# Two graph blocks on one core: the left sums, the normalisation and three orders in the front

## What is computed

```
h = max(layernorm(x), 0)
type_sum_a = adj @ h ; type_sum_b = adj @ h
attn_a = sigmoid(concat(type_sum_a, h) @ Wa.T + ba)      # attn_b the same with Wb, bb
H = h @ W_sa
s_left, s_right = H @ a_sa[0, :256], H @ a_sa[0, 256:]
e = where(adj != 0, exp(-leaky_relu(s_left[:, None] + s_right[None, :], 0.01)), 0)
x_a = (e / (sum(e, 1) + 1e-5)) @ H
x_b = adj @ (h @ W_gcnb) + b_gcnb
x = x + sigmoid(attn_a * x_a + attn_b * x_b)
```

## Time and profile before

| | |
|---|---|
| median of 3 runs | 1577.26 us |
| the profiled execution, its own time | 1576.58 us |
| its span, first to last instruction | 1574.8 us |
| PE busy | 1542.0 us, 98% |
| DVE / ACT / POOL busy | 72% / 68% / 62% |
| granted TensorE clock, mean | 1.000 |

### The profile page before, as it was taken

The page is one execution under the profiler, slowest core; times in us unless marked ns, Lnnn a source line. Parts: engine busy times, 40 slices in busy tenths (PEclk is TensorE's granted clock), DMA queues, the critical chain, the costliest instruction groups (busy, mean ns, idle before and its releaser), DMA issues.

```text
span 1574.8 us, 34791 instructions
## 1 busy us (share of the span) xinstructions
PE 1542.0 (98%) x12902; PEld 1532.8 (97%) x12902; DVE 1138.9 (72%) x2145; ACT 1067.3 (68%) x2085; POOL 969.6 (62%) x864
## 2 busy tenths in 40 slices
PE   6999999999999999999999999999999999999998
PEld 5999999999999999999999999999999999999997
DVE  7766666666666577778777778766777777777774
ACT  4579889988985566666666666645666666666666
POOL 2112222222220288888888888846888888888885
PEclk9999999999999999999999999999999999999999
DMA  4124444454441034344444435522343344434343
GB/s 151 48 61 118 125 115 119 119 147 120 115 115 35 24 95 105 105 105 106 107 108 105 105 105 161 204 68 75 105 105 105 105 105 105 105 105 105 105 107 106
DMA packets 95034, 166.27 MB, mean 106 GB/s; under 512 B 12816, under 2 KB 25743, under 8 KB 94607
## 3 DMA queue, kind: packets, MB, share of 16 engines
q1 hardware_dynamic: 66816, 116.17, 27.2%
q0 software_dynamic: 24336, 44.31, 11.5%
q10 hardware_dynamic: 3710, 3.56, 0.7%
HBM read 150.87 MB, written 13.13 MB: 104 GB/s over the span
## 4 chain that ended last, share of the span: by engine, by line
PE 89%; issue 3%; DVE 3%; POOL 2%; ACT 1%; DMA 1%; SPq 0%; POOLq 0%; DVEq 0%; ACTq 0%
PE PS L1295 33%; PE PS L1507 9%; PE PS L1510 9%; PE PS L1509 9%; PE PS L1370 5%; PE PS L1367 5%; PE PS L1369 5%; PE PS L1368 5%; PE PS L1366 5%; POOL FR L508 1%; POOL X L501 1%; DVE ROW L837 0%; DVE AF L1104 0%; DMA X<-xt 0%; PE PS L1538 0%
## 5 line engine op out<-in xcount | busy, mean ns | idle before, releaser
L508 POOL TENSOR_TENSOR FR<-AF,FR 128x512 fp32r<-128x512 f32 x338 | 451.1, 1335 | 122.3 <-ACT FR L703 114.6
L1295 PE MATMUL PS<-FR,RB 128*128 128x256 f32 x3900 | 514.0, 281 | 1.8 <-ACT X L657 1.7
L1295 PEld LDWEIGHTS PS<-FR,RB 128*128 128x128 f32 x3900 | 481.9, 188 | 3.0 <-ACT X L657 3.0
L501 POOL TENSOR_TENSOR X<-X,ROW 128x512 f32<-128x512 f32 x283 | 370.7, 1310 | 82.0 <-ACT ROW L713 82.0
L1507 PE MATMUL PS<-FR,RA 128*128 128x256 f32 x1300 | 370.6, 285 | 2.5 <-POOL FR L508 2.3
L1510 PE MATMUL PS<-FR,RA 128*128 128x256 f32 x1300 | 365.0, 281 | 0.0
L1509 PE MATMUL PS<-FR,RA 128*128 128x256 f32 x1300 | 364.4, 280 | 0.0
L1104 DVE TENSOR_TENSOR AF<-PS,AJ 128x512 f32<-128x512 f32 x338 | 231.0, 683 | 56.3 <-ACT PS L669 46.2
L466 POOL DMA_DIRECT2D STGT<-adjt x169 | 90.1, 533 | 293.0 <-PE PS L1370 293.0
L1036 DVE TENSOR_TENSOR AF<-PS,AF 128x512 f32<-128x512 f32 x286 | 196.4, 687 | 100.7 <-PE PS L1295 98.4
L657 ACT ACTIVATE X<-PS 128x512 f32<-128x512 f32 x272 | 162.3, 597 | 156.4 <-DVE AF L1036 149.5
(11 more groups left out here) (174 smaller groups left out, 2424.1 us busy)
## 6 DMA issues: line engine op xcount, KB each, us to landing
AJ<-adjt SPq DMA_DIRECT2D x338, 256.0 KB, 2.7
STGT<-adjt POOLq DMA_DIRECT2D x169, 256.0 KB, 3.0
xt_scratch<-ROW SPq DMA_DIRECT2D x12, 512.0 KB, 2.6
RB<-xt_scratch SPq DMA_DIRECT2D x12, 512.0 KB, 6.2
x_scratch<-X ACTq DMA_DIRECT2D x13, 256.0 KB, 2.1
ROW<-x_scratch SPq DMA_DIRECT2D x13, 256.0 KB, 3.3
out<-ROW SPq DMA_DIRECT2D x12, 256.0 KB, 3.5
ROW<-rec_scratch SPq DMA_DIRECT2D x22, 128.0 KB, 3.7
```

The source lines that it names most:

```text
L501: nc.gpsimd.tensor_tensor(slot, slot, MB.unsqueeze(1).broadcast_to([P, 2, 256]), ALU.subtract)\
L508: nc.gpsimd.tensor_tensor(LO[g % 2], WA[g % 2], HI[g % 3].bitcast(F32), ALU.subtract)\
L1295: last = nc.tensor.matmul(out, stationary(a, k), moving(b, k), start=(k == 0 and i == 0), stop=(k == K - 1 and i == 2))
```

## The change

- **Left sums.** `products_l` goes, and WSL with it. The vector W_sa @ a_left becomes a fourth extra column of H's weights (HX was 260 already), so s_left comes out as a column of H's product, and `h2_low` copies four columns to XS instead of three. s_left then stands down the partitions and has to be laid along the free axis. For pair 0 that is done by ACT (`spread_left`), two transposes on PE (`turn_left`, bank 1) and a copy on ACT. For pairs 1 to 6 and 7 to 12 it is done by two stores of SL to DRAM and two loads back with the partitions broadcast, on SP's queue (`SL_PARTS`).
- **Banks.** `turn` hands out five turns a pair; transposes of pair 1 use bank 0.
- **Weight vectors.** The two sums go from DVE (reduce_sum) to ACT (four copies with an accumulated output, written into the weights).
- **Normalisation** of pairs 2 to 12 goes from DVE to POOL, between the powers and the loads of adjacency units. Pairs 0 and 1 stay on DVE.
- **x's second part** goes ahead of a_sa's rows on SP's queue; its statistics are taken in two parts. In the passes, statistics move ahead of `h2_low`.
- **Leaky steps.** In pass 1 `leaky0(0)` and `exp0(0)` come after G's high parts. After the loop, `leaky0(13)` is no longer issued right there; for units 11 to 13 the order is leaky n + 2, high n + 1, exp n + 2, then back to the old one. In pass 12 both copies of XS come before the low parts.

```diff
+SL_PARTS = [(1, 7), (7, PAIRS)]
+N_LATE = UNITS + 1
...
         def turn(pr, i):
-            return 6 * pr + i + 1 if i else max(6 * pr - 5, 0)
+            return 5 * pr + i + 1 if i else max(5 * pr - 4, 0)
...
             sp.dma_start(WRAW0[:, :, 0:GX + D + 2], wx).then_inc(w_in, 16)
+            sp.dma_start(X[:, X_PARTS[1][0]:X_PARTS[1][1], :], xt[:, X_PARTS[1][0]:X_PARTS[1][1], :])\
+              .then_inc(x_in[1], 16)
             sp.dma_start(AROW, rows[:, 0:2 * D]).then_inc(row_in, 16)
...
+            for i, (p0, p1) in enumerate(SL_PARTS):
+                sp.wait_ge(sr_done, 2 * p1)
+                sp.dma_start(sl_dram[2 * P * p0:2 * P * p1].rearrange("(t p o) -> p t o", p=P, o=1),
+                             SL[:, 2 * p0:2 * p1, :], allow_slow_non_contiguous=True).then_inc(sl_st, 16)
+                sp.wait_ge(sl_st, 16 * (i + 1))
+                sp.dma_start(SLB[:, 2 * P * p0:2 * P * p1],
+                             sl_dram[2 * P * p0:2 * P * p1].partition_broadcast(P)).then_inc(sl_in[i], 16)
...
             for n in range(NSTG):
                 load_unit(n)
-            for n in range(2, len(LN_PARTS)):
-                inverse_root(n, *LN_PARTS[n])
-            for n in range(UN - NSTG):
+            normalise(2)
+            for p in range(1, PAIRS - 2):
+                if p - 1 in LN_CHAIN:
+                    i = LN_CHAIN[p - 1]
+                    inverse_root(i, *LN_PARTS[i])
+                normalise(p + 2)
+                if p >= 2:
+                    load_unit(p - 2 + NSTG)
+            for n in range(PAIRS - 4, UN - NSTG):
...
+            def spread_left():
+                act.wait_ge(sr_done, 2)
+                nc.scalar.activation(PEB[:, :, 0:P], SL[:, 0:2, :].broadcast_to([P, 2, P]), ACT.Copy).then_inc(sl_spread, 1)
...
+                for k in range(K):
+                    wa = (PEB, PAB)[side][:, k, 0:D]
+                    last = nc.scalar.activation(wa, wa, ACT.Copy, accum_out=WRAW0[:, k, c:c + 1])
...
+                ahead = pr == PAIRS - 1
+                if not (ahead and h):
+                    dve.wait_ge(h2hi_done, t + 1 + ahead)
+                    for i in range(1 + ahead):
+                        nc.vector.tensor_copy(XS[:, t + i, :], PS[:, bank_of(pr, 3 + h + i), D:D + 4])\
+                          .then_inc(sr_done, 1)
...
-            def products_l(pr):
...
+            def turn_left():
+                pe.wait_ge(sl_spread, 1)
+                for h in range(2):
+                    last = nc.tensor.transpose(PS[:, 1, h * P:(h + 1) * P], PEB[:, h, 0:P], IDN[:, :])
+                last.then_inc(sl_mm, 1)
```

More of the change, by code:

```diff
@@ L212, in two_graph_blocks @@
         wv_zero = sem("wv_zero")
-        wv_step = sem("wv_step")
-        wsl_hi = sem("wsl_hi")
+        wv_done = sem("wv_done")
+        sl_spread = sem("sl_spread")
+        sl_mm = sem("sl_mm")
+        sl_first = sem("sl_first")
+        sl_st = sem("sl_st")
+        sl_in = [sem(f"sl_in{i}") for i in range(len(SL_PARTS))]
         wh_cast = sem("wh_cast")
@@ L471, in inverse_root, with normalise @@
                 nc.gpsimd.tensor_tensor(LNT[:, 1, t0:t1], LNT[:, 0, t0:t1], NHALF[:, 0:t1 - t0], ALU.pow)                  .then_inc(ln_pow, 1)
+            def normalise(pr):
+                pool.wait_ge(ln_done, next(i for i, (t0, t1) in enumerate(LN_PARTS) if 2 * pr + 1 < t1) + 1)
+                if pr:
+                    pool.wait_ge(tp_done, pr)
+                for h in range(2):
+                    t = 2 * pr + h
+                    last = nc.gpsimd.tensor_scalar(HN[:, h, :], X[:, t, :], RSTD[:, t:t + 1], NMR[:, t:t + 1],
+                                                   ALU.mult, ALU.add)
+                last.then_inc(hn_done, 1)
             pool.wait_ge(half_set, 1)
@@ L544, in leaky0 @@
                 pr, u = n // UNITS, n % UNITS
-                act.wait_ge(slb_done, pr + 1)
+                if pr == 0:
+                    act.wait_ge(sl_first, 1)
+                else:
+                    act.wait_ge(sl_in[next(i for i, (p0, p1) in enumerate(SL_PARTS) if pr < p1)], 16)
                 act.wait_ge(sr_done, 2 * u + 2)
@@ L601, in _ @@
             transposed_high(0)
-            act.wait_ge(wv_step, 1)
-            nc.scalar.activation(WSL[:, 0, :, :], WV[:, 0, :].unsqueeze(2).broadcast_to([P, K, P]), ACT.Copy)\
-              .then_inc(wsl_hi, 1)
-            act.wait_ge(wv_step, 3)
+            for side in range(2):
+                act.wait_ge(wv_pool, side + 1)
+                c = GX + D + 3 - side
+                for k in range(K):
+                    wa = (PEB, PAB)[side][:, k, 0:D]
+                    last = nc.scalar.activation(wa, wa, ACT.Copy, accum_out=WRAW0[:, k, c:c + 1])
+            last.then_inc(wv_done, 1)
+            act.wait_ge(wv_done, 1)
             act.wait_ge(wv_zero, 1)
@@ L956, in _ @@
             normalise(0)
+            dve.wait_ge(x_in[1], 16)
+            statistics(2, 4)
             dve.wait_ge(wg_hi, 1)
@@ L1002, in _ @@
                     statistics(t0, t1)
+                if p == 1:
+                    mask0(0)
+                h2_low(p, 0)
+                if p >= 1:
+                    low0(p - 1)
+                h2_low(p, 1)
                 if p in LN_CHAIN:
                     i = LN_CHAIN[p]
-                    variances(i, *LN_PARTS[i], 2 + sum(b <= LN_PARTS[i][1] for a, b in LN_STATS.values()))
+                    variances(i, *LN_PARTS[i], 3 + sum(b <= LN_PARTS[i][1] for a, b in LN_STATS.values()))
             mask0(UNITS - 1)
```

124 lines of the change are left out of this document (56 added, 68 removed).

## The result

| | before | after |
|---|---|---|
| median (4 runs each, same chip) | 1577.45 us (1576.45 to 1577.85) | 1568.12 us (1567.39 to 1568.53) |
| ratio, 95% interval | | 0.9943 (0.9927 to 0.9959) |
| profiled execution, its span | 1576.58, 1574.8 us | 1568.53, 1566.7 us |

The change is faster by 9.3 us (0.6%). The forecast was 15.65 us faster, and the time lies 1.1 us above the range. The profiled execution stands 0.4 us above the median. The mean granted TensorE clock was 1.00 in both profiles.

A forecast was written before the change was run, and what follows sets the result against it. TensorE, busy 98% of the span, was taken to bound the kernel. Savings of 8.1 (first passes), 5.6 (full passes) and 1.95 (end of the front), together 15.65, took 1577.26 to 1561.6 us; range 1558.5 to 1567.0.

The forecast's parts named there:

- unknown cost: Price of one 128x256 tensor_scalar on POOL, shown by no row: taken as 0.7 us, between 0.33 and 1.46.
- Term 3, the end of the front: PE's idle before unit 12, at 104.54 us, would vanish: -1.95 us.
- high to 3.7, low to 4.4: Times after the last H product for unit 12's high and low parts, under the 4.8 us PE has in units 10 and 11.
- now both copies come right behind the high parts: In pass 12, both XS copies would be done 0.8 us after the last H product.
- the rival on the store: Slow word stores of s_left make leaky 13 27 us late, with PE waiting: 1588 us; chance 0.04.
- at nothing: Parts priced at no cost, among them the second s_left store and load, due over 100 us later.
- the end of the front keeps its wait: PE's wait before unit 12 stays because DVE or the first s_left load is a little late: 1563.6 us; chance 0.12.
- Term 1: Full passes 6 to 12, units 3 to 10: each loses the left product's 0.80 us on PE, -5.6 us.
- Term 2: First passes, up to unit 3: the new order starts unit 0 at 26.7 and unit 3 at 44.85, -8.1 us.
- G starts at 11.35: Pair 0's first G product on PE would start at 11.35 us, against 11.62 before.

The follow-up runs named there:

- low_first: Changed kernel, but after the loop DVE takes the low parts of units 12 to 14 ahead of the masks of units 13 to 15; 1571.53 us.
- lows: row_late with DVE's low parts of units 12 to 14 before the next masks, and low 11 ahead of the XS copies in pass 12; 1565.62 us.
- g_twice: Changed kernel with G's first product made twice in passes 6 to 12, six matmuls more each; 1570.68 us.
- pow_first: Changed kernel, but POOL takes the power of part 1 (pairs 1 and 2) between its two weight products; 1569.23 us.
- row_late: row_store with the first small transpose moved from the start of pass 7 to the middle of G's products in pass 8; 1565.87 us.
- row_store: Changed kernel with s_left turned on PE and copied by ACT, so each store writes 12 rows of 512 B instead of 1,536 words; 1567.78 us.
- rows_first: Changed kernel with a_sa's rows again ahead of x's second part on SP's queue; 1570.38 us.
- rows_low_first: row_store with DVE's low parts of units 12 to 14 ahead of the masks of units 13 to 15; 1566.28 us.
- norm_dve: Changed kernel with pairs 2 to 12 normalised on DVE again; 1572.91 us (11 runs).

## Why the prediction failed where it did

What held: less work on PE moved the end; POOL normalised without holding the passes; most of the shape of the first passes (pair 2 turned at 17.54, forecast 17.3; pair 3 at 23.24 with a wait of 1.40, forecast 22.65 and 1.8); and behind the front the first block moved rigidly (the second drifted by about 1 us in the profiled pair). The unknown cost came out at 0.55: 22 tensor_scalar of 128x256 on POOL took 545 to 1112 ns, median 558, half the shorter product as the nearest row had it. The estimate of 0.4 from the Trainium skill ("GPSIMD Engine Reference", "Elementwise — side-by-side cycle accounting", 1.8 cycles an element) was too low, and 0.7 was too high. It barely mattered.

- **Term 3, the end of the front: forecast -1.95, came out at +1.7.** This is the step that failed most, 3.6 of the 6.4 us that are missing. First, the chain "high to 3.7, low to 4.4" followed ACT's new order and never asked in which order DVE takes masks and lows. DVE's program had mask 13 ahead of low 12, so the wait for exp 13 was still there, one engine further on; low_first shows it. Second, "now both copies come right behind the high parts" moved them past low 11, and PE idles 0.64 before unit 11, a wait that the kernel before didn't have (lows takes it out). The two waits, 0.64 and 1.48, add up to the old 2.12: nothing was won there. Third, the stall of 1.50 at unit 15 is the rival on the store in another place. I priced the store for the one who reads its result, leaky 13, with 35 us of slack, and never for those who share the DMA engines with it. The second store I put "at nothing" for the same reason, and just that one cost: 1.50 here, up to 3.9 in others. It costs PE this much because low 15 stands behind mask 16 on DVE; no run put low 15 first. The rival "the end of the front keeps its wait", at 0.12, named DVE and the right wait, but it counted on a little delay and kept the rest of the sum. (In the rival on the stores, 61 against 35 leaves 26, not 27; nothing hangs on it.)
- **Term 1: seven times 0.80, measured 4.2 in all.** The 0.80 was read from one start to the next. Six matmuls at 0.12 are 0.72; g_twice adds just about that. The other 0.08 lies behind the transposes whatever follows; over seven passes that is 0.56 too much. A further 0.57 went in one pass, between units 4 and 5, which I took to be PE-bound since before it was; the last 0.25 is spread, most of it over the two passes beside it. Three rows of POOL and DVE speak of it:

```profile
50.57 1.67 POOL L486 TENSOR_TENSOR LNT<-LNT,COL 128x8 f32<-128x8 f32 x1 [0.90 <-DVE LNT L905]
```
```profile
52.34 0.47 DVE L912 TENSOR_TENSOR LNT<-LNT 128x8 f32<-128x8 f32 x1 [0.29 <-POOL LNT L486]
...
53.05 0.34 DVE L916 SCALAR_TENSOR_TENSOR LNT<-LNT 128x8 f32<-128x8 f32 x1
```

  PE itself waits in that pass for the low parts of H (`DVE RA L954: 0.4, 2` from 54 to 60 us). The power for eight columns comes late in the pass, and DVE does the scales ahead of a mask and a low part that PE needs, stretched by POOL's normalise beside them (0.47 and 0.34 where such an instruction takes 0.16). That this is the cause is read from the rows; no run took it away.
- **Term 2: unit 0 at 27.75, forecast 26.7; unit 3 1.4 late.** The step that failed first is "G starts at 11.35" (12.29), and H, forecast at 15.05, followed at 15.72: I had read the exclusion from the earlier trace rows, and cited it, but charged it to POOL's product alone. It holds DVE as well, 0.75 on an instruction ahead of `transposed_low` (L934). pow_first brought 0.6 of it back, counted to unit 0. The rest, 0.45 between the turning of pair 3 and unit 0 and 0.35 up to unit 3, I haven't split further.

## What to carry to other kernels

Reorder a chain on one engine only after writing down the order of every engine that hands it on: the wait that leaves one queue often stands in the next. Price a slow transfer twice, once for its reader and once for every other transfer that is in flight beside it. And before a small store is put on the critical side of a kernel, turn its data so that it leaves in rows: a transpose and a copy cost PE and ACT almost nothing where nobody waits for them (row_late), and 1.6 us where somebody does (row_store). Last, when a variant comes out slower than its stall explains, look at the granted clock behind the stall before explaining the rest.

## What the runs showed of the hardware

- **Single-word stores to DRAM end late, whatever their size.** 1,536 words took 10.2 to 13.1 us (from the store's issue to that of the load that waits for it), 256 words 11.0 in the median from 20 to 54 us and 8.9 from 54 to 100, and 12 rows of 512 B 1.3 to 2.5. By the packet records of the changed kernel the words' own packets were through about 2 us after the issue.
- **They slow the loads of the same core meanwhile.** Twice the packet time for the same 720 packets (50.2% against 25.9%); loads of 256 KB with a median of 3.0 took 5.7 in the median from 84 to 104 us and up to 11.5. The Trainium skill, "DMA: Bandwidth & Descriptors", "Specifications", says that below 512 B a transfer becomes a read-modify-write. The rows of 512 B and the words lie on the two sides of that limit, and they differ; where the limit lies no run here shows. That the words delay others is only in these runs.
- **Stalls of this kind scatter.** The stall at unit 15 was 1.5 to 3.9 us in four kernels (the changed one, rows_first, low_first, pow_first) that started unit 11 within half a microsecond of each other. low_first and pow_first lost by it, and by the clock behind it, more than they had won.
- **A wait of PE can cost its length and then the clock.** The granted clock was 0.50 behind a stall of 3.88 (low_first), one of 2.21 (pow_first), a wait of 1.82 (rows_low_first) and one of 1.26 with another of 0.96 before it (norm_dve); each time this cost 1.4 to 1.5 us more. It stayed at 1.00 behind stalls of 1.50 (the changed kernel) and 2.85 (rows_first) and behind the same 1.82 in row_store. So the length of the wait alone doesn't decide it. Each kernel has one trace, so whether its other executions lost the same isn't known.
- **A four-column instruction on DVE can cost 0.92.** In the ten traces where POOL's second product runs beside it, it is held until that product ends, so where it falls counts, not what it does.
